# Strassen weight preparation between the queue's other duties, two kinds of tiles on GpSimd, and a group's loads spread over it

## The reference

```python
mod = (silu(c) @ wmod).reshape(4, 6, 1, -1)          # sa, ca, ga, sb, cb, gb
h = layernorm(x) * (1 + ca) + sa
x = x + ga * attn(h, wq, wk, wv, wo)                 # 32 q heads, 8 kv heads of 128, RoPE, causal window of 256
h = layernorm(x) * (1 + cb) + sb
x = x + gb * moe_lora(h, gate_w, lora_A, lora_B)     # 8 experts of rank 64, top 2, softmaxed gate
```

## Time and profile before

| | us |
|---|---|
| median of 3 runs (lowest, highest) | 2777.93 (2777.42, 2781.24) |
| profiled execution | 2775.14 |
| its span | 2773.3 |
| TensorE busy in it | 2546.4 (92%) |
| VectorE, ScalarE, GpSimd busy | 1824.9, 1168.5, 896.4 |

### The profile page before, as it was taken

One profiled execution on the slowest core, in us unless ns is written; L12 is line 12 of the kernel. 1 busy time (PEld: TensorE's weight loads), 2 busy tenths in 40 slices (PEclk: granted clock), 3 DMA queues, 4 the chain that ended last, 5 costly groups with the idle time before them and its releaser, 6 DMA issues.

```text
span 2773.3 us, 42764 instructions
## 1 busy us (share of the span) xinstructions
PE 2546.4 (92%) x12281; PEld 2095.7 (76%) x12281; DVE 1824.9 (66%) x4818; ACT 1168.5 (42%) x2781; POOL 896.4 (32%) x974
## 2 busy tenths in 40 slices
PE   7999999999697679885969999999999999999999
PEld 5888888888576567774757778778878887787887
DVE  7777766677465545664657877667677776776653
ACT  4555554544332323332235555334344443345341
POOL 0333333312233342553353323233133333331112
PEclk9999999999898889997989999999999999999999
DMA  8766665695735645565857666555776767547411
GB/s 345 281 234 231 239 227 215 216 347 202 251 126 179 231 145 190 194 222 191 320 167 229 223 220 214 197 182 187 274 271 227 243 235 266 194 155 278 166 69 61
DMA packets 332545, 599.66 MB, mean 216 GB/s; under 512 B 20688, under 2 KB 211984, under 8 KB 330896
## 3 DMA queue, kind: packets, MB, share of 16 engines
q1 hardware_dynamic: 327968, 582.08, 59.7%
q10 hardware_dynamic: 4464, 16.25, 1.6%
HBM read 439.89 MB, written 158.38 MB: 216 GB/s over the span
## 4 chain that ended last, share of the span: by engine, by line
PE 66%; issue 9%; DMA 7%; DVE 7%; POOL 6%; ACT 3%; SPq 2%; DVEq 0%; POOLq 0%; ACTq 0%
PE bank L1079 20%; PE bank L1081 20%; PE bank L1080 20%; DMA raw<-in_wo 3%; PE bank L1243 3%; POOL mix_lo L980 1%; DVE acc L1686 1%; DMA hT_lo_scratch<-l_lo 1%; SPq L569 1%; DVE swapped L1647 1%; DVE rotated L1650 1%; POOL mix_hi L978 1%; POOL mix_lo L973 1%; POOL mix_lo L976 1%; POOL mix_lo L974 1%
## 5 line engine op out<-in xcount | busy, mean ns | idle before, releaser
L1426 ACT ACTIVATE prob<-prob,nbias 128x256 f32<-128x256 f32 (+1 forms) x512 | 247.0, 483 | 382.2 <-DVE nbias L1717 228.7
L1079 PE MATMUL bank<-hT_hi,w_q_hi 128*128 128x512 f32 x912 | 367.8, 403 | 9.3 <-DVE swapped L1647 9.3
L1081 PE MATMUL bank<-hT_hi,w_q_lo 128*128 128x512 f32 x912 | 357.1, 392 | 0.0
L1080 PE MATMUL bank<-hT_lo,w_q_hi 128*128 128x512 f32 x912 | 356.7, 391 | 0.0
L1061 POOL TENSOR_TENSOR rotated<-v_all 128x256 f32<-128x256 f32 x64 | 47.6, 765 | 853.2 <-DVE v_all L1757 853.2
L1243 PE MATMUL bank<-ident_t,prob 128*128 128x128 f32 x896 | 186.5, 281 | 147.8 <-DVE prob L1727 146.4
L1079 PE MATMUL bank<-w_o_hi,qo_hi 128*128 128x512 f32 x744 | 299.3, 402 | 11.3 <-DVE acc L1670 9.3
L1074 POOL TENSOR_TENSOR pT<-pT,lower_t 128x256 fp32r<-128x256 f32 x256 | 195.8, 767 | 296.4 <-DVE pT L1751 296.0
L1081 PE MATMUL bank<-w_o_hi,qo_lo 128*128 128x512 f32 x744 | 291.5, 392 | 0.0
L1080 PE MATMUL bank<-w_o_lo,qo_hi 128*128 128x512 f32 x744 | 290.9, 391 | 0.0
L1243 PEld LDWEIGHTS bank<-ident_t,prob 128*128 128x128 f32 x896 | 123.3, 143 | 186.7 <-DVE prob L1727 165.0
(11 more groups left out here) (296 smaller groups left out, 6271.1 us busy)
## 6 DMA issues: line engine op xcount, KB each, us to landing
w_q_hi<-w_q_hi_scratch SPq DMA_DIRECT2D x82, 512.0 KB, 7.5
w_q_lo<-w_q_lo_scratch SPq DMA_DIRECT2D x82, 512.0 KB, 8.2
w_o_hi<-w_o_hi_scratch SPq DMA_DIRECT2D x68, 512.0 KB, 8.6
w_o_lo<-w_o_lo_scratch SPq DMA_DIRECT2D x68, 512.0 KB, 9.4
w_s_hi_scratch<-mix_hi SPq DMA_DIRECT2D x28, 640.0 KB, 3.7
w_s_lo_scratch<-mix_lo SPq DMA_DIRECT2D x28, 640.0 KB, 5.3
stage<-in_wq SPq DMA_DIRECT2D x32, 512.0 KB, 4.5
stage<-in_wo SPq DMA_DIRECT2D x32, 512.0 KB, 5.3
```

The source lines that it names most:

```text
L1079: eng.matmul(o, st[0], mv_[0], start=start, stop=False)
L1080: eng.matmul(o, st[0], mv_[1], start=False, stop=False)
L1081: return eng.matmul(o, st[1], mv_[0], start=False, stop=stop)
L1426: eng.activation(tile, tile, ACT.Exp, bias=nbias[:, u:u + 1], scale=-1.0, accum_out=rowsum[:, u:u + 1]).then_inc(s_exp, 1)
```

## The change

In batch 1, two of the preparation steps, the tile's store and a third step stand ahead of the w_o fetch (without a tile: three steps ahead, one behind). At the entry of batch 2, three steps stand ahead of w_o, and only products 4 and 1 are fetched there. In paired groups, products 4 and 1 are reloaded where they were, and 3, 5, 2, 7, 6 in the next group, by the counts of V and of the transposes of its attention. The turned tile's two operations and low part, and the LoRA low parts, go from DVE to GpSimd, behind the last sum of a paired group (batch 1's tiles stay on DVE). ScalarE's tile work moves into the first Q rope, the LoRA highs ahead of it.

```diff
@@ sp_enter
-            mix(0)
+            for i in range(3):
+                mix(i)
             eng.wait_ge(s_wo, wo_at(n, b) + 1)
-            for i in (4, 1, 5, 2):
+            eng.wait_ge(s_mixd, WS_KEPT + 32 * PIECES)
+            for i in (4, 1):
                 sp_mixed(eng, i, n % KV)
-            mix(1)
-            mix(2)
+            mix(3)
             eng.wait_ge(s_proj, 6 * n + 6)
             sp_head(eng, 0, (n + 1) % KV)
             sp_head(eng, 3, (n + 1) % KV)
-            for i in (7, 6):
-                sp_mixed(eng, i, n % KV)
-            mix(3)
-            eng.wait_ge(s_proj, 6 * n + 7)
-            sp_mixed(eng, 3, n % KV)
@@ sp_paired_group
-            g = n % KV
+            g, gm = n % KV, m % KV
+            eng.wait_ge(s_proj, 6 * m + 7)
+            sp_mixed(eng, 3, gm)
+            eng.wait_ge(s_T, UNITS * m + 4)
+            sp_mixed(eng, 5, gm)
+            eng.wait_ge(s_T, UNITS * m + 6)
+            sp_mixed(eng, 2, gm)
             eng.wait_ge(s_proj, 6 * n + 2)
             sp_head(eng, 1, g)
+            eng.wait_ge(s_T, UNITS * m + 11)
+            sp_mixed(eng, 7, gm)
+            eng.wait_ge(s_T, UNITS * m + 13)
+            sp_mixed(eng, 6, gm)
...
-                for at, i in enumerate(ORDER):
-                    if i != 3:
-                        eng.wait_ge(s_wo, done + len(ORDER) + at + 1)
-                        sp_mixed(eng, i, g)
+                for i in (4, 1):
+                    eng.wait_ge(s_wo, done + len(ORDER) + ORDER.index(i) + 1)
+                    sp_mixed(eng, i, g)
...
-                eng.wait_ge(s_proj, 6 * n + 7)
-                sp_mixed(eng, 3, g)
@@ sp_groups, batch 1
+                    def beside():
+                        sp_turned_row(eng, b, t)
+                        sp_mix(eng, 3 * t, [piece(3 * t + i) for i in range(3)])
+                        sp_tile_store(eng, b, t)
+                        sp_mix(eng, 3 * t + 2, [piece(3 * t + i) for i in range(2, 4)])
                     sp_turned_load(eng, b, t)
-                    sp_direct_group(eng, n, b, lambda: sp_turned_row(eng, b, t))
-                    sp_mix(eng, 3 * t, [piece(3 * t + i) for i in range(4)])
-                    sp_tile_store(eng, b, t)
+                    sp_direct_group(eng, n, b, beside)
                 with eng.Fori(1 + QT, KV) as g:
-                    sp_direct_group(eng, b * KV + g, b)
-                    sp_mix(eng, 4 * g - 8, [piece(i, g - 2) for i in range(5)])
+                    sp_direct_group(eng, b * KV + g, b, lambda: sp_mix(eng, 4 * g - 8, [piece(i, g - 2) for i in range(4)]))
+                    sp_mix(eng, 4 * g - 5, [piece(i, g - 2) for i in range(3, 5)])
                 return
+            if b == PAIRED:
+                eng.wait_ge(s_mixd, WS_KEPT + 32 * PIECES * (KV - 1))
@@ p1_pool, behind the sums of a paired group
+                with eng.Fori(0, QT) as g:
+                    pool_paired_group(eng, b * KV + g, b)
+                    if b < BATCH - 1:
+                        pool_turned_tile(eng, b * QT + g)
+                    else:
+                        for slot in range(2):
+                            pool_lora_lo(eng, g + 1, slot)
+        def pool_turned_tile(eng, i):
+            j = i - QT
+            xt = stage[1][:].rearrange("p (k n) -> p k n", n=P)
+            rstd, shift = (stage[0][:, z:2 * P:2].unsqueeze(1).broadcast_to([P, KT, P]) for z in range(2))
+            eng.wait_ge(s_turned, 48 * (j + 1))
+            eng.tensor_tensor(xt, xt, rstd, ALU.mult).then_inc(s_lxn, 1)
+            eng.wait_ge(s_lxn, QT + 2 * j + 1)
+            eng.tensor_tensor(xt, xt, shift, ALU.add).then_inc(s_lxn, 1)
+            eng.wait_ge(s_lhi, i + 1)
+            eng.tensor_tensor(l_lo[:], lf[:], l_hi[:].bitcast(F32), ALU.subtract).then_inc(s_llo, 1)
@@ act_paired_project (new, for act_project in batches 2 and 3)
+            act_rope(eng, n, 0, False, lambda: act_highs(eng, n - 1, b, ((1, 1), (1, 7), (1, 6))))
+            if pair is not None:
+                for slot in range(2):
+                    eng.wait_ge(s_lr[slot], 16 * pair)
+                    eng.activation(lora[slot][0][:], stage[slot][:].rearrange("p (k n) -> p k n", n=P), ACT.Copy).then_inc(s_rhi, 1)
+            def beside_first():
+                if tile is not None:
+                    act_tile(eng, tile, range(KT), True)
+                    act_tile_hi(eng, tile)
+            act_rope(eng, n, 1, False, beside_first, b)
@@ dve_paired_group
-                if turned is not None and r == 3:
-                    dve_tile_lo(eng, turned)
                 dve_rope(eng, n, r)
-                if turned is not None and r == 1:
-                    dve_turned_tile(eng, turned)
                 if g is not None and r == 1:
                     dve_tile2(eng, g)
-                if g is not None and r in (2, 3):
-                    dve_lora_lo(eng, g, r - 2)
```

More of the change, by code:

```diff
@@ L1456, in act_project_split, with act_project @@
             eng.wait_ge(s_hst, 32 * (tile + 1))
-        def act_project(eng, n, batch_done=None, tile=None, part=None, pair=None, b=None):
-            act_rope(eng, n, 0, False, (lambda: act_highs(eng, n - 1, b, ((1, 1), (1, 7), (1, 6)))) if b is not None else lambda: None)
+        def act_project(eng, n, batch_done=None, tile=None):
+            act_rope(eng, n, 0, False)
             for r in range(1, 1 + GQ):
-                if part == 2 and r == 3:
-                    eng.wait_ge(s_mm1, KT * (part + 1))
-                    eng.activation(part_row, bank[LATE_BANK[part]][:, 0:256], ACT.Copy).then_inc(s_mr1, 1)
                 stored = {1: (0, 1, 2), 2: (3,)}.get(r, ()) if batch_done is not None else ()
-                act_rope(eng, n, r, False, lambda: act_store_x1(eng, batch_done, stored), b)
+                act_rope(eng, n, r, False, lambda: act_store_x1(eng, batch_done, stored))
                 if r <= 2 and tile is not None:
@@ L1470, in act_project, with act_paired_project @@
                         act_tile_hi(eng, tile)
-                if r <= 2 and pair is not None:
-                    eng.wait_ge(s_lr[r - 1], 16 * pair)
-                    eng.activation(lora[r - 1][0][:], stage[r - 1][:].rearrange("p (k n) -> p k n", n=P), ACT.Copy).then_inc(s_rhi, 1)
+            if tile is not None:
+                eng.wait_ge(s_hst, 32 * (tile + 1))
+        def act_paired_project(eng, n, b, tile=None, part=None, pair=None):
+            act_rope(eng, n, 0, False, lambda: act_highs(eng, n - 1, b, ((1, 1), (1, 7), (1, 6))))
[4 more added lines that the diff above has]
+            def beside_first():
+                if tile is not None:
+                    act_tile(eng, tile, range(KT), True)
+                    act_tile_hi(eng, tile)
+            act_rope(eng, n, 1, False, beside_first, b)
+            for r in range(2, 1 + GQ):
+                if part == 2 and r == 3:
+                    eng.wait_ge(s_mm1, KT * (part + 1))
+                    eng.activation(part_row, bank[LATE_BANK[part]][:, 0:256], ACT.Copy).then_inc(s_mr1, 1)
+                act_rope(eng, n, r, False)
             if tile is not None:
@@ L1604, in act_groups @@
         def act_groups(eng, b, ln):
-            paired = b >= PAIRED
-            sums_b = b if paired else None
+            if b < PAIRED:
+                with eng.Fori(1, 1 + QT) as g:
+                    n = b * KV + g
+                    act_attention(eng, n - 1, b, tail=lambda: act_tile_sqrt(eng, b * QT + g - 1))
+                    act_project(eng, n, tile=b * QT + g - 1)
+                with eng.Fori(1 + QT, KV) as g:
+                    n = b * KV + g
+                    act_attention(eng, n - 1, b)
+                    act_project(eng, n)
+                act_attention(eng, b * KV + (KV - 1), b, ln)
+                return
             if b == PAIRED:
@@ L1610, in act_groups @@
                 n = b * KV + g
-                act_attention(eng, n - 1, b, tail=lambda: act_tile_sqrt(eng, b * QT + g - 1) if ln else None, paired=paired)
-                act_project(eng, n, tile=b * QT + g - 1 if ln else None, pair=None if ln else g, b=sums_b)
+                act_attention(eng, n - 1, b, tail=lambda: act_tile_sqrt(eng, b * QT + g - 1) if ln else None, paired=True)
+                act_paired_project(eng, n, b, tile=b * QT + g - 1 if ln else None, pair=None if ln else g)
                 if not ln:
@@ L1622, in act_groups @@
                     n = b * KV + g
-                    act_attention(eng, n - 1, b, paired=paired)
-                    act_project(eng, n, part=g - QT if g - QT < 3 else None, b=sums_b)
+                    act_attention(eng, n - 1, b, paired=True)
+                    act_paired_project(eng, n, b, part=g - QT if g - QT < 3 else None)
             act_attention(eng, b * KV + (KV - 1), b, ln)
@@ L1883, in dve_tile_lo @@
             eng.tensor_tensor(l_lo[:], lf[:], l_hi[:].bitcast(F32), ALU.subtract).then_inc(s_llo, 1)
-        def dve_lora_lo(eng, g, slot):
```

(3 more changed lines are left out.)

10 lines of the change are left out of this document (7 added, 3 removed).

## The result

The changed kernel takes 2638.96 us (2635.69 to 2642.16, 4 runs); the kernel before, beside it on the same chip, 2778.99 us. The ratio is 0.9495, with a 95% interval of 0.9479 to 0.9512: faster by 5%. The forecast was 2626, 13.0 us too low. The profiled spans are 2773.3 before and 2635.6 after: 137.7 less, where the terms of the forecast add up to 151.7.

What follows compares the result with a forecast made beforehand. SyncE's queue order was taken to cause the waits in batch 1. Five terms sum to 151.7 us, from 2775.1 to 2623.4; with 2.8 for the median the forecast is 2626 us, range 2598 to 2666.

Steps and rivals of the forecast that it cites:

- Term 1: Four tile groups of batch 1: ScalarE's wait for the tile's store goes, 76.0 us a group, 90.4 us saved (70 to 101).
- landing takes 5.3 us: Batch 1's tile groups: a stored low part lands in 5.3 us, so the second piece is stored 10 to 11 us after Q+0.
- rival B: Batch 1's tile groups: landing takes 10 us instead of 5.3, w_o comes 5 us late in four groups; 2654 us, chance 0.11.
- rival A: Q ropes on DVE are held by low parts on GpSimd through the SBUF exclusion, overlaps exposed; 2665 us, chance 0.13.
- Term 2: Three groups of batch 1 without a tile: last piece stored sooner, 74.6 us a group, 16.9 us saved (7 to 26).
- Term 3: Change of batch: hT reload's wait 28.88 to 8.3 us, batch 2's entry hole 24.69 to 14.4; 30.9 us saved.
- Term 4: Four paired tile groups of batch 2: TensorE's waits for `swapped` go, 3 us given back for overlap; 7.5 us (-2 to 11).
- Term 5: Batch 3: LoRA low parts moved to GpSimd mostly remove four waits at the start of attention; 6 us (0 to 8.5).
- Rival D: Paired groups: product 6's spread weights land later than 16 us, TensorE waits in 14 groups; 2808 us at 13 us; chance 0.03.
- E: Batch 1: the tile's store stays behind GpSimd in the queue and the wait stays; 2778 us, chance 0.02.
- DVE beside GpSimd: DVE's addition takes 3.29 us beside GpSimd, 0.68 with it idle; a low part holds a rope up to its whole length, mostly hidden.

Runs made afterwards that it cites:

- order_only: The kernel before with only SyncE's new order of duties in batch 1: 2678.87 us against 2778.78, ratio 0.9648.
- late_wait: The changed kernel with ScalarE's wait for all prepared weights moved to its first copy of an attention output in batch 2: 2629.17 us, ratio 0.9462.
- queue_only: The kernel before with all of SyncE's changes, spread loads too, but the engines' work as before: 2652.10 us, ratio 0.9546.
- burst_loads: The changed kernel with the paired groups' mixed weights loaded in one stretch as before: 2660.39 us, ratio 0.9572.

## Why the prediction was right, and where it was off

**What bounds the kernel: right.** SyncE's order made the holes of batch 1; that order alone gives 99.9 us (order_only).

**Term 1, 90.4: measured 63.8, 64 to 69 over the five profiles of this stage.** The mechanism is right and the size wrong. A group took 82.6 us instead of 76.0. In the profile after, TensorE is idle 31.84 us in the four groups (330.55 - 298.71): the 1.93 for DVE's sum four times (forecast), 4.02 at the start of attention four times (2.05 forecast, a row from a group without a tile; the tile groups of before had 2.75 to 3.52), 5.2 for w_o (none), 2.9 ahead of V (none). The other term is slower work: 298.71 busy against 4 x 71.27, so 3.4 us a group where I gave 0.6 for clock dips. The granted clock, the third figure from the right in the windows, shows at least part of it, here in the 4 us behind the wait of 4.02:

```profile
810.45:814.58 4.13, 4.13 (x15) 3.44 (x16) 2.14 (x11) 1.31 (x6) 0.00 (x0) 0.60 1.00 293
```

The step that failed is "landing takes 5.3 us", and with it the start of the chain: the broadcast is out at Q-3.1, where the forecast took over the Q-5.6 of before, so the first store is 1.3 us later than its latest forecast; landing takes 2.4 longer, and from there every piece, and w_o behind them, about 5 to 6.5 us late (the tile's store only 2). That is rival B's place (w_o is late next), in a size of 1.3 to 2.3 us a group, and beside it rival A's mechanism, DVE held by GpSimd's low part, exposed on the last rope of the group only. Both were given as alternatives to the forecast, where each was a part of it. That the total still came within 0.5% is in part luck: the paired groups gave back 25.5 of the 40.7 that were missing, 8.6 of them in groups that the forecast left out.

**Term 2, 16.9: measured 14.8.** Groups of 75.3 where 74.6 was said.

**Term 3, 30.9: measured 18.9.** The reload's hole is 12.08 (8.3 forecast) and the entry's 18.67 (14.4); waits of 2.41 and 2.02 at two starts of attention, not forecast, take the other 4. The reload went out 39.3 us behind that group's Q+0 (1175.64), not 35: the first of its four pieces is stored at Q-5.3, where a last store at Q+34 wanted Q-8, and the three steps to the last take 43.1 us, not 42. late_wait shows that somewhat under half of the entry's hole (18.67 to 10.22) is the place of ScalarE's wait, which the forecast had not questioned.

**Term 4, 7.5: measured 17.2, and 12 to 17 over the four profiles of this stage.** The waits were counted right: TensorE idles 0.53 us there (275.80 - 275.27) instead of 11.07 (292.98 - 281.91), 10.5 less. I took off 3 of it for an overlap that cost nothing, and put at nothing the 6.6 us by which TensorE's busy time fell. GpSimd's 128x1024 operations, forecast at 2.7, take 2.40 to 2.44, and the overlap is there but hidden, as GpSimd's and DVE's timelines in a tile group of batch 2 show:

```profile
1510.72 2.40 POOL L992 TENSOR_TENSOR l_lo<-lf,l_hi 128x1024 fp32r<-128x1024 f32 x1 [4.40 <-ACT l_hi L1553]
```

```profile
1511.19 2.48 DVE L1721 TENSOR_TENSOR qo_lo<-rotated,qo_hi 128x512 fp32r<-128x512 f32 x1 [1.14 <-ACT qo_hi L1454]
```

The groups run at some 69 us without a TensorE wait of 1 us. queue_only, with the tile on DVE and ScalarE's old order, has none of this gain: the engines' moves are the cause.

**Term 5, 6: measured 13.2, and the reason was wrong.** I put it down to the LoRA low parts' move. queue_only has the gain without the move, burst_loads the move without the gain. The cause is the spread of the loads, which I costed at nothing: the bursts had held back the LoRA stores that ScalarE waits for. I had put TensorE's waits at the start of attention down to DVE, whose `prob` is their releaser in the timeline; one step back stands ScalarE's exp, which waits 4.75 to 5.83 us for a LoRA store each time. The next three groups gain 8.6 us the same way: ScalarE's one wait for `mod_scratch<-lf` there falls from 8.4 to 0.9 us.

**Rival D, spread loads too late, and E, no effect: both excluded.** TensorE waits for no `w_s` load in the paired groups of batch 3 (busy 274.43 of 274.66).

**DVE beside GpSimd: the conclusion right, the comparison wrong.** The 0.68 us that I set against DVE's addition of 3.29 is a product with an operand from PSUM (L1646), which takes 0.69 beside GpSimd too. The addition itself, undisturbed, stands two rows on in the kernel before:

```profile
1615.97 0.69 DVE L1650 TENSOR_TENSOR rotated<-rotated,swapped 128x512 f32<-128x512 f32 x1
```

## What to carry to other kernels

In a queue that serves several engines in order, sum up the chain to the last one with the landings as they will be behind the new neighbours, not with the median of the page, and find the last user on it (here w_o, then the reload): every microsecond added to a step in front is paid there, and what another engine gains meanwhile is waited away in front of it. Put what has the nearest consumer ahead of what has slack (w_o ahead of the third piece, 10.4 us), and place a wait for "everything is prepared" at the first instruction that needs it (9.8 us). Bursts of loads cost something even where none of them is late, if a small store with a waiting consumer lands behind them.

## What the runs showed of the hardware

- GpSimd and DVE hold each other up in both directions. Over batch 1 of after, DVE's addition of two SBUF tiles (L1709) takes 1216 ns in the mean of 40, against 0.69 us undisturbed; with memsets in place of the low part 854 ns (L1712 there). GpSimd's 128x256 sums take 0.74 us, or 1.18 beside such operations (1116.20 in after). DVE's product with one operand from PSUM (L1705) stays at 691 ns, and at 692 with the memsets. The Trainium skill ("SBUF — State Buffer", section "Who interferes with whom") says that, of additions and products like these (`tensor_tensor`), only a DVE operation with two SBUF inputs contends, and only with a GpSimd one that reads SBUF. The trace agrees, with the 691 ns and with the 0.69 us beside the memsets.
- Splitting one GpSimd operation of 128x1280 into five of 128x256 raised it from 2.91 to 4.36 us.
- The 640 KB store of a low part landed in 5.0 to 5.6 us with only its high part issued close ahead, in 7.4 to 8.0 behind a broadcast and two raw loads issued within 2.4 us ahead of it (four tile groups of after), and in 12.3 to 12.7 behind the eight w_o loads and two raw loads (four of before).
- In the 4 us behind TensorE's four waits of 4.0 us the granted clock was 0.50, 0.60, 0.59 and 0.50, and from 909.07 to 913.20, around the end of the 2.3 us for w_o at 909.46, 0.64: all or most of those stretches at the lower level, 1.2 GHz. Behind the 1.6 us at 826.50 and the 1.9 at 857.02 it stayed at 1.00.
